# A two-layer gated attention and mixture kernel: the first mixture's shared expert written out in place of loops, and three moves in the first attention's order

## The reference

```
x = x + tanh(g_xattn[0]) * L0_xattn(layernorm(x), ctx, ctx)          # 16 heads of 16
x = x + tanh(g_ffn[0])   * L0_ffn(layernorm(x))                      # ternary weights
x = x + tanh(g_xattn[1]) * L1_xattn(ctx, layernorm(x))               # 8 heads of 128
x = x + tanh(g_ffn[1])   * L1_ffn(layernorm(x))                      # top 2 of 8, capacity
```

```
def _bit_quant(W):                                    # each weight becomes -s, 0 or +s
    scale = clip(mean(abs(W), axis=-1, keepdims=True), 1e-05)
    return clip(round(W / scale), -1, 1) * scale

h = (x - mu) / sqrt(var + eps) * gamma + beta
shared_out = silu(h @ bit_quant(shared_w1).T) @ bit_quant(shared_w2).T   # every token
probs = softmax(h @ router_w.T); top_idx = argmax(probs)
routed_out = silu(h @ bit_quant(expert_w1[top_idx]).T) @ bit_quant(expert_w2[top_idx]).T * max(probs)
return shared_out + routed_out
```

## Time and profile before

| | |
|---|---|
| device time, 3 runs | 1070.16 us median (1065.31 to 1075.05) |
| the profiled execution | 1069.45 us, span 1067.7 us |
| PE busy | 956.3 us (90%), mean granted clock 0.944 of full speed |
| DVE, ACT, POOL busy | 768.2 us (72%), 621.9 us (58%), 230.4 us (22%) |
| `attention_0` | 0 to 198.5 us of the span |
| `front_0` | 198.5 to 266.9 us; its shared expert from about 224 us |
| rest of the program | 266.9 to 1067.7 us |

### The profile page before, as it was taken

One profiled execution on the slowest core, in us unless ns is written; L12 is line 12 of the kernel. 1 busy time (PEld: TensorE's weight loads), 2 busy tenths in 40 slices (PEclk: granted clock), 3 DMA queues, 4 the chain that ended last, 5 costly groups with the idle time before them and its releaser, 6 DMA issues. The chain is left out here.

```text
span 1067.7 us, 22058 instructions
## 1 busy us (share of the span) xinstructions
PE 956.3 (90%) x7942; PEld 881.4 (83%) x7942; DVE 768.2 (72%) x1919; ACT 621.9 (58%) x1502; POOL 230.4 (22%) x289
## 2 busy tenths in 40 slices
PE   5899997787997789999999999999978999799992
PEld 4788885676776579999999999999968999699992
DVE  7898886674666697887677676766776877466665
ACT  4788885374885555555555555555538444466560
POOL 3443442023001520000000101010000000566642
PEclk9899997688898799999999999999989999899996
DMA  8511110002562300000000000003024000534517
GB/s 272 188 61 60 44 61 2 2 25 69 178 162 69 73 23 20 2 21 1 21 1 21 2 21 1 21 2 99 1 76 123 1 2 1 134 129 138 148 56 266
DMA packets 68121, 69.24 MB, mean 65 GB/s; under 512 B 14512, under 2 KB 59696, under 8 KB 67888
## 3 DMA queue, kind: packets, MB, share of 16 engines
q1 hardware_dynamic: 61520, 52.89, 16.2%
q0 software_dynamic: 5376, 14.69, 4.8%
q10 hardware_dynamic: 1120, 0.27, 0.1%
HBM read 46.07 MB, written 21.76 MB: 64 GB/s over the span
## 5 line engine op out<-in xcount | busy, mean ns | idle before, releaser
L1558 PE MATMUL a_psK<-a_kvThi,a_wk 128*128 128x512 f32 x256 | 97.4, 421 | 4.9 <-issue 2.6
L314 POOL TENSOR_SCALAR t_neg<-t_raw,t_nthr 128x256 bf16<-128x256 f32 (+1 forms) x54 | 60.7, 1139 | 106.4 <-DVE t_nthr L543 100.4
L1617 PE MATMUL a_psY<-a_nwhi,a_uhi 128*128 128x256 f32 x256 | 73.8, 288 | 5.1 <-DVE a_ulo L1790 5.1
L1677 ACT ACTIVATE a_probs<-a_psS,a_softmax 128x256 f32<-128x256 f32 x128 | 59.6, 471 | 29.6 <-DVE a_softmax L1772 29.6
L1667 ACT ACTIVATE a_khi<-a_psK,a_bk 128x512 fp32r<-128x512 f32 x64 | 44.1, 688 | 50.1 <-PE a_psK L1558 49.4
L1689 ACT ACTIVATE a_uhi<-a_psU 128x512 fp32r<-128x512 f32 x64 | 38.3, 598 | 58.8 <-PE a_psU L1598 58.7
L1598 PE MATMUL a_psU<-a_pTlo,a_tokhi 128*128 128x256 f32 x256 | 72.4, 283 | 0.0
L1598 PE MATMUL a_psU<-a_pThi,a_tokhi 128*128 128x256 f32 x256 | 72.4, 283 | 0.0
L1598 PE MATMUL a_psU<-a_pThi,a_toklo 128*128 128x256 f32 x256 | 72.4, 283 | 0.0
L1617 PE MATMUL a_psY<-a_nwlo,a_uhi 128*128 128x256 f32 x256 | 72.3, 282 | 0.0
L1617 PE MATMUL a_psY<-a_nwhi,a_ulo 128*128 128x256 f32 x256 | 72.2, 282 | 0.0
(11 more groups left out here) (394 smaller groups left out, 3203.3 us busy)
## 6 DMA issues: line engine op xcount, KB each, us to landing
t_raw<-in_L_ffn_expert_w SPq DMA_DIRECT2D x16, 512.0 KB, 3.5
f_raw<-in_fc_T SPq DMA_DIRECT2D x16, 512.0 KB
m_results<-a_zeros SPq DMA_DIRECT2D x8, 512.0 KB
m_sorted<-m_zeros SPq DMA_DIRECT2D x1, 2944.0 KB, 12.6
m_n<-m_sorted SPq DMA_DIRECT2D x23, 128.0 KB, 2.4
m_expert_out<-e_y SPq DMA_DIRECT2D x23, 128.0 KB, 2.2
a_rawkv<-in_L_xattn_Wkv SPq DMA_DIRECT2D x8, 256.0 KB, 3.4
m_n<-in_sh_T SPq DMA_DIRECT2D x2, 1024.0 KB, 7.8
```

The lines of the kernel that those rows point to most:

```text
L314: ins = pool.tensor_scalar(neg[:, own], raw[h % NRAW][:, own], nthr[h % 2][:, n:n + 1], None, ALU.is_lt)
L1558: ins = pe.matmul(psK[:].rearrange("p b t -> p (b t)"), wk[x][:, a, h * DH:(h + 1) * DH], kvT[pair % 2][y][:, a, :, :, :].rearrange("p b m ...
L1617: ins = pe.matmul(psY[:, b, :], u[ch % 2][x][:, f, hh * P:(hh + 1) * P], nw[y][:, f, 2 * j + hh, :], start=first, stop=last, skip_group_ch ...
L1677: act.activation(probs[n % 2][:, b, :], psS[n % 2][:, b, :], ACT.Exp, bias=nmax[:, n % NM, b:b + 1], accum_out=sums[:, n % NM, b:b + 1]).t ...
```

## The change

Three edits in `attention_0` and three in `front_0`.

1. DVE, t = 16: `signs(17)`, the context statistics and the first 8 norm steps move behind `residual(13)` and `heads_out(14)`. At t = 17 the other 8 norm steps move from ahead of `residual(14)` to between `residual(14)` and `heads_out(15)`.
2. PE, t = 0: `turn_half(0)` moves behind `scores(1, 0)`.
3. The three `Fori` loops of the shared expert become Python loops, so that every pass is written out with constant addresses and semaphore values.

```diff
@@ attention_0, VectorE, step(t)
-                    if t >= 1 and due(t + 1):
+                    if t >= 1 and due(t + 1) and t < NB:
                         signs(t + 1)
...
-                    if NB <= t < NB + 2:
-                        if t == NB:
-                            k.step(dve.bn_stats(c_stats[:, NB - 1, :], ctx_sb[:, NB - 1, :]))
-                        for n in range((t - NB) * 8, (t - NB + 1) * 8):
-                            k.step(norm_step(dve, n, *both))
                     if there(t - 3):
                         residual(t - 3)
+                    if t == NB + 1:
+                        for n in range(8, 16):
+                            k.step(norm_step(dve, n, *both))
                     if there(t - 2):
                         heads_out(t - 2)
+                    if t == NB:
+                        signs(t + 1)
+                        k.step(dve.bn_stats(c_stats[:, NB - 1, :], ctx_sb[:, NB - 1, :]))
+                        for n in range(8):
+                            k.step(norm_step(dve, n, *both))
@@ attention_0, TensorE, step(t)
-                    if due(t):
+                    if due(t) and t > 0:
                         turn_half(t)
                     scores(t + 1, 0, t - 1, 1)
+                    if t == 0:
+                        turn_half(t)
@@ front_0, TensorE, ScalarE, VectorE
-                with pe.Fori(1, PAIRS // 2 - 1) as i:
+                for i in range(1, PAIRS // 2 - 1):
...
-                with act.Fori(1, PAIRS // 2) as i:
+                for i in range(1, PAIRS // 2):
...
-                with dve.Fori(2, PAIRS // 2) as i:
+                for i in range(2, PAIRS // 2):
```

## The result

| | before | after |
|---|---|---|
| device time, median of 21 runs each | 1072.06 us | 1064.61 us |
| the profiled execution | 1069.45 us, span 1067.7 | 1062.3 us, span 1060.2 |
| mean granted clock of PE | 0.944 | 0.951 |

Run by run in the same rounds, in which both kernels are timed, the ratio is 0.9952, with a 95% interval of 0.9934 to 0.997: about 5.1 us less (3.2 to 7.1), half of the 10.2 us forecast. The time itself, 1064.61 us, lies in the range given.

A forecast was written before the change was run, and what follows sets the result against it. It took attention_0 to be bound by the chain through DVE, and the shared expert by TensorE until ScalarE's waits broke the ring. 2.2 + 0 + 8.0 = 10.2 us less gave 1060.0 us for the median, range 1055.0 to 1067.0.

The forecast's parts named there:

- part 3: Shared expert: loops written out remove register instructions, branches and two table loads; 8.0 us, ends 2.6 and 8.5.
- ScalarE's 5.40 us before silu(6): Shared expert: wait without a recorded releaser after the loop's second jump back; expected to go, silu(6) at 246.8, not 254.85.
- Part 1: End of attention_0: DVE's reordering starts heads_out(15)'s reciprocal 3.2 us sooner, less 0.9 for output(15); 2.2 us taken.
- the 0.2 us that I put on a hand-over: End of attention_0: added after weigh(14) finished at 182.14, so DVE's block could begin at 182.3.
- Rival C: Clock stays low after the idle 4.6 us; 192 matmuls cost 18.6 us more, total 1078.6 us; chance 0.04.
- the ring: Shared expert's engines working pair after pair; forecast to end near 258 us, or 276 at the low clock.
- Part 2: Start of attention_0: scores(1, 0) fills TensorE's idle time, but DVE then waits for POOL at signs(2); 0 us.
- the end of 0.3 that I gave: Start of attention_0: the edit's worst case, 0.3 us lost because PE does turn_half(0) a little later.
- rival A: Shared expert: long waits come from scatter time and stay; only table loads give 2.6 us, total 1065.4; chance 0.20.

The follow-up runs named there:

- e8: Kernel before with only the start edit (scores(1, 0) ahead of turn_half(0)); one execution, 1048.7 us.
- e13: Changed kernel plus eight matmuls of output's size in TensorE's idle time ahead of output(15); ratio to before 0.9991 (0.997 to 1.0013).
- e9: Kernel before, unchanged, profiled again on a second chip; one execution, 1054.73 us.
- e3: Kernel before with only the shared expert's three loops written out; ratio to before 0.9963 (0.9943 to 0.9982), 4.0 us less.
- e4: Kernel before with only VectorE's new order at the end of the first attention; ratio to before 0.9975 (0.9942 to 1.0009).
- e10: Changed kernel, unchanged, timed again on a chip where before takes 1053.3 us; ratio to before 0.9999 (0.9974 to 1.0023).
- e5: Changed kernel, unchanged, run once more on a chip where before takes 1053.3 us; one execution, 1059.39 us.
- e11: Changed kernel with the old start, scatters on four semaphores and norm steps spread 4, 8, 4 in the tail; ratio to before 0.995 (0.993 to 0.997).
- e2: Changed kernel with 48 always-met waits added to ScalarE's stream ahead of silu(0); one execution, 1067.86 us.
- e7: Changed kernel with the scatters counted on four semaphores instead of two; ratio to before 0.9993 (0.9972 to 1.0015).

## What the prediction had right, and the step that failed

The step that failed is part 3's: it takes ScalarE's 5.40 us before silu(6) for a cost of the hardware loop and books 8.0 us for writing it out. The waits came back in straight code (4.02 and 2.06 us) and were nearly gone in the loop on a quiet chip; written out, the loops are worth 1.0 us there. Part 1 missed, besides, what the low clock can cost behind the stage.

**Part 1, the tail: right in its place, incomplete behind it.** Among profiles with a low-clock stretch of 10 us the old tail takes 35.2, 35.2, 36.0 and 36.0 us, the new one 33.0, 33.0, 32.9, 32.9, 32.8 and 33.2: 2.6 us less, forecast 2.2. Without the stretch it is 31.1 (e8) against 28.6, 2.5. output(15) at 1.97 to 2.08 us was charged for. (The 0.2 us that I put on a hand-over from TensorE to DVE was my estimate: in the trace of before, DVE started 0.04 to 0.28 us behind the end of the matmul that it had waited for, 0.07 us in the median of 61 such waits, and 0.07 us here, from weigh's last matmul to the reciprocal; it changes nothing.) What I missed is that the low clock that begins in the 4.86 idle us (at 189.0 us) need not end with output(15): in four of eight profiles it lasted through the router's part and took 4.1 us back (26.2 us against 22.1). Rival C named this mechanism, but put it into the ring, with a chance of 4%. Half of 4.1 leaves 0.5 us of the 2.6; but no timed run confirms this price, as e13 shows.

**Part 2, the start: right in its mechanism.** signs(2) at 35.78 was released by POOL after 2.04 us, as forecast. It costs 0.4 us in the mean of the profiles, just outside the end of 0.3 that I gave; what costs it was not looked for.

**Part 3, the loops: the step that failed.** With "silu(6) starts when the first half of up(6) is done, at 246.8, not at 254.85" I put the 5.40 us down to the loop, since they stood behind its jump back. (By my own 0.117 us a matmul that half is done at 246.5; nothing hangs on the 0.3.) The straight code waited as well, 4.02 and 2.06 us, and the loop on a quiet chip waits 1.80 us (e9) and not 5.40: the wait is that for TensorE's signals, and they can be late in either code. Of the 8.0 us that I gave the part, 1.0 us is what the written-out code is worth where no signal is late. That a jump back of the loop can cost such a wait is shown by no run, and the straight code has no branch there. My rival A, that the waits are those of the scatters' time, is what the changed kernel's profile showed. It had a chance of 0.20. That the stage came out 2.8 us shorter beside its 2.6 is luck, since the two profiles also differ in how late their signals were. Its price was too high as well: undisturbed, the two table loads and the register work are worth 1.0 us. A load of 1.28 us delays ScalarE by that much, but TensorE, which sets the pace, then waits only 0.57 us before down(4) (0.58 in e9). In the same way it is luck that e3's stage was 8.0 us shorter, as forecast: some 7 of them are the jam that it did not have.

The evidence that I had and passed over: up(6)'s row was over long before silu(6) began, and the row said "remote" and not the loop. A signal can stand up to 6.6 us behind the modelled end of its matmul (up(6), in both profiles; 0.01 to 0.02 us on the quiet chips). The semaphore events show that, and no row of the timeline does; what held the signals up these runs don't tell.

**The sum.** Undisturbed chips: -2.6 for the tail, +2.1 for half of the long stretches, +0.4 for the start, -1.0 for the ring: 1.1 us less, against the -0.1 and -2.0 us measured. On the chips with late signals the change measured 5.1 us less, the loops alone 4.0 and the tail alone 2.7, with 2 to 4 us of uncertainty each. The ring there took 39.3, 32.9 and 37.9 us with loops and 36.8, 36.1 and 30.6 without, so some 2.2 us less in the mean, which three profiles of each can't prove. With that in place of the 1.0 the sum is 2.3 us; with the long stretch in one of the four profiles of the new tail there (e4), and not in half, it is 3.4, inside 3.2 to 7.1 but under the 5.1. What made up the rest is not known.

**Open.** Whether it is GpSimd's scatters that hold TensorE's signals up, why on some chips and not on others, and why the signals turn late only 8 to 20 us behind the first scatter. Whether the recording of the trace takes part in it: late signals are seen only where a trace was recorded, and only profiles that have them lack the records of some signals (1 to 4 of the 32, in five of the six). Whether the written-out code suffers less from it. Why the low-clock stretch lasted 14 us in e10 and 24 us in e5. Why e3's gain was partly given back: its last stage, from the first `f_psX<-ident,rows` matmul on, took 279.3 us against 274.5 in before, and in the seven profiles of the slower chips this stage took anything from 273.1 to 279.3 us.

## What to carry over

Before a stall is put down to the code it stands in, look at what was done long before it and still released it late, and take the kernel's profile twice, if possible on two chips; a wait that comes and goes is not the code's. Small steps without near dependences belong behind the work that another engine waits for, not ahead of it: moving the same steps was worth 2.6 us in one place and 4.5 in the other (a tail of 35.6 us in the mean to 33.0 and to 31.1), and in e11 PE did its last projection at a granted clock of 1.00 (1.13 us against 1.97). An edit that lets PE stand still for almost 5 us can be paid again in the stage behind, as the profiles have it in four of eight cases.

## What the runs showed of the hardware

- TensorE's signals can be late in the time in which GpSimd issues indirect DMAs: all six profiles with scatters beside the ring on chips where before takes 1068 to 1072 us have them late (at most by 0.6 to 6.6 us, and by 0.6, 1.5 and 6.0 on one and the same chip, in e3, e4 and e2), twelve on two chips where it takes 1053 to 1055 us have none over 0.02. That the DMAs cause it is argued from the times and not shown.
- The chips differ elsewhere too: from GpSimd's first gather of routed rows in the last stage (`rows<-m_tokens`) to the first expert matmul (`f_psH<-m_turned`) it took 15.5 to 15.7 us on the slower ones, 11.5 to 14.3 on the others.
- Two executions of one kernel on one chip (e10, e5) had low-clock stretches (a granted clock of 0.50) of 14 and of 24 us from the same point of the program.
- An indirect DMA of 128 rows mostly took GpSimd 0.97 us (up to 1.49 for some), with 0.30 between two; with at most two on their way beside the ring it also waited for landings (up to 2.3 us at once, e2 and e10), with four every gap was 0.30 or 0.31 us (e7).
